# Attention and gated LoRA layer on one core: mask and maximum in one VectorE pass per head, third group's probabilities normalized by VectorE

## The reference, cut to what matters

```python
x = x + attn(layernorm(x), wq, wk, wv, wo, q_norm_w, k_norm_w)
x = x + ffn(layernorm(x), weight, gate_w, lora_U, lora_V)

# attn: 16 heads of 64, 4 key/value heads, window of 128 tokens
q, k = rmsnorm(q), rmsnorm(k)
scores = einsum("bqhd,bkhd->bhqk", q, k) / sqrt(64)
scores = where((i >= j) & (i - j < 128), scores, -inf)
y = einsum("bhqk,bkhd->bqhd", softmax(scores), v) @ wo.T
# ffn: 8 experts of rank 16
gate = softmax(xt @ gate_w.T)
out = xt @ weight.T + einsum("ne,eor,ner->no", gate, lora_V, t) / 16
```

## Time and profile before

| | |
|---|---|
| median of the runs | 2353.57 us (2352.46 to 2354.76, 3 runs) |
| the profiled execution | 2355.66 us |
| its span, first to last instruction | 2353.9 us |
| TensorE matmuls busy | 2311.7 us, 98% |
| VectorE busy | 2129.8 us, 90% |
| ScalarE busy | 2051.7 us, 87% |
| GpSimd busy | 1262.7 us, 54% |
| mean granted TensorE clock | 0.997 |

### The profile page before, as it was taken

How to read it: one execution, slowest core, us unless ns; L and a number is a source line. 1 busy time by engine, 2 the same in 40 slices (tenths; PEclk the granted TensorE clock), 3 DMA queues, 4 the chain that set the end, 5 groups by cost and what they waited for, 6 DMA issues and landing times.

```text
span 2353.9 us, 117523 instructions
## 1 busy us (share of the span) xinstructions
PE 2311.7 (98%) x49424; PEld 1979.1 (84%) x49424; DVE 2129.8 (90%) x5871; ACT 2051.7 (87%) x7175; POOL 1262.7 (54%) x1644
## 2 busy tenths in 40 slices
PE   6999999999999999999999999999999999999998
PEld 4888888888888888888888888888888888888886
DVE  6899999999999999999999999999999999999996
ACT  5888888898888988888888889888888888898886
POOL 2555555555555555555555555555555555555553
PEclk9999999999999999999999999999999999999999
DMA  2000000000000000000000000000000000000000
GB/s 73 12 17 21 17 16 17 21 16 17 21 17 17 17 21 17 17 17 21 17 16 21 17 16 17 21 17 17 17 21 17 16 18 20 17 16 21 17 10 14
DMA packets 39913, 44.25 MB, mean 19 GB/s; under 512 B 4448, under 2 KB 38624, under 8 KB 39392
## 3 DMA queue, kind: packets, MB, share of 16 engines
q1 hardware_dynamic: 39392, 36.73, 5.0%
HBM read 19.93 MB, written 16.78 MB: 16 GB/s over the span
## 4 chain that ended last, share of the span: by engine, by line
PE 75%; ACT 14%; DVE 9%; issue 1%; POOL 0%; DMA 0%; SPq 0%; DVEq 0%
PE ps_a L676 9%; PE ps_scores L721 9%; PE ps_y L743 7%; PE ps_d L670 5%; ACT probs L345 5%; PE ps_d L672 5%; PE ps_d L671 5%; PE ps_y L756 4%; PE ps_c L676 4%; PE ps_y L773 4%; PE ps_b L670 3%; PE ps_b L672 3%; PE ps_b L671 3%; DVE gate L577 2%; PE ps_b L676 2%; ACT qT L333 2%
## 5 line engine op out<-in xcount | busy, mean ns | idle before, releaser
L345 ACT ACTIVATE probs<-merged,neg_max 128x128 f32<-128x128 f32 x2048 | 801.2, 396 | 102.8 <-DVE neg_max L515 99.5
L242 POOL TENSOR_TENSOR q_r<-q_ve,minus_half 128x8 f32<-128x8 f32 x256 | 420.3, 1642 | 264.2 <-DVE q_ve L491 257.9
L345 ACT ACTIVATION_READ_ACCUMULATOR probs<-merged,neg_max 128x1 f32 x2048 | 397.3, 194 | 0.0
L721 PE MATMUL ps_scores<-kT,qT 64*32 64x160 f32 (+4 forms) x16384 | 377.5, 281 | 5.4 <-DVE merged L509 4.2
L515 DVE TENSOR_REDUCE neg_max<-merged 128x4 f32<-128x512 f32 x512 | 343.7, 671 | 0.1
L264 POOL TENSOR_SCALAR_AFFINE_SELECT pT_other<-pT 128x256 f32<-128x256 f32 x384 | 159.5, 415 | 342.7 <-ACT pT L352 338.8
L352 ACT ACTIVATE pT<-ps_a 128x512 f32<-128x512 f32 x512 | 307.6, 601 | 12.0 <-PE ps_a L676 1.6
L676 PE MATMUL ps_a<-ident,probs 128*128 128x128 f32 x2048 | 314.8, 276 | 1.1 <-DVE probs L526 0.6
L670 PE MATMUL ps_d<-wo_h,yT_h 128*128 128x256 f32 x1024 | 310.4, 303 | 0.7 <-ACT qT L333 0.7
L672 PE MATMUL ps_d<-wo_l,yT_h 128*128 128x256 f32 x1024 | 288.0, 281 | 0.0
L671 PE MATMUL ps_d<-wo_h,yT_l 128*128 128x256 f32 x1024 | 287.6, 281 | 0.0
(11 more groups left out here) (119 smaller groups left out, 6347.4 us busy)
## 6 DMA issues: line engine op xcount, KB each, us to landing
xs<-x SPq DMA_DIRECT2D x128, 128.0 KB, 2.1
out<-ob SPq DMA_DIRECT2D x128, 128.0 KB, 2.1
w_plain<-w_qkv SPq DMA_DIRECT2D x3, 512.0 KB, 4.9
w_plain<-w_o SPq DMA_DIRECT2D x8, 128.0 KB, 5.4
w_plain<-w_ffn SPq DMA_DIRECT2D x1, 392.0 KB, 6.2
w_plain<-w_v SPq DMA_DIRECT2D x1, 128.0 KB, 5.1
nw<-norm_w SPq DMA_DIRECT2D x1, 1.0 KB, 5.4
```

The lines of the kernel that those rows point to most:

```text
L242: pool.tensor_tensor(q_r[:, T % DEEP, c], q_ve[:, T % DEEP, c], minus_half[:, 0:8], ALU.pow).then_inc(s_qr[n], 1)
L345: last = nc.scalar.activation(probs[:, r, h], merged[:, r, h], ACT.Exp, bias=neg_max[:, r, h:h + 1], accum_out=den[:, r, h:h + 1])
L721: last = nc.tensor.matmul(ps_scores[queries, 2 * half + c, first:end], qT[rows, T % 2, 2 * g + c, queries], kT[rows, g // 2, at + first:at ...
```

## The change

For tiles of slot 0, `merge` becomes one `tensor_tensor_reduce` for each of the four heads. It writes the negated masked scores, -(scores + neg_later), to `merged` and their minimum over the keys, which is the negated maximum, to `neg_max`. `maximum` no longer runs for these tiles, and `exps` waits for `s_merged` instead of `s_max` and undoes the sign with scale -1. The semaphore `s_max` counts the tiles of slot 1 to 3 alone.

`NORM_BY_POOL` becomes empty: the normalization of group 2 leaves GpSimd for VectorE, in all 128 tiles, and stands between `high_value_difference(T)` and `gate_share(T - 3)`.

```diff
-NORM_BY_POOL = (2,)
+NORM_BY_POOL = ()
@@ gpsimd, step
                 q_power(T + 2, 0)
-                norm_by_pool(T, 2)
                 select(T, 1)
@@ scalar, exps
-                    act.wait_ge(s_max, groups(T, g))
+                    if slot(T):
+                        act.wait_ge(s_max, later_groups(T, g))
+                    else:
+                        act.wait_ge(s_merged, groups(T, g))
                     for h in heads:
-                        last = nc.scalar.activation(probs[:, r, h], merged[:, r, h], ACT.Exp, bias=neg_max[:, r, h:h + 1], accum_out=den[:, r, h:h + 1])
+                        last = nc.scalar.activation(probs[:, r, h], merged[:, r, h], ACT.Exp, bias=neg_max[:, r, h:h + 1], scale=1.0 if slot(T) else -1.0,
+                                                    accum_out=den[:, r, h:h + 1])
@@ vector, merge
                         dve.wait_ge(s_s, groups(T, g))
-                        nc.vector.tensor_tensor(merged[:, ring(T, g)], ps_scores[:, :, P:2 * P], neg_later[:].unsqueeze(1).to_broadcast(every),
-                                                ALU.add).then_inc(s_merged, 1)
+                        r = ring(T, g)
+                        for h in range(REP):
+                            last = nc.vector.tensor_tensor_reduce(merged[:, r, h], ps_scores[:, h, P:2 * P], neg_later[:], -1.0, -MASKED, ALU.add, ALU.min,
+                                                                  accum_out=neg_max[:, r, h:h + 1])
+                        last.then_inc(s_merged, 1)
@@ vector, maximum
-                if live(T):
+                if live(T) and slot(T):
@@ vector, step
                 high_value_difference(T)
+                norm_probs(T - 1, 2)
                 gate_share(T - 3)
```

## The result

The changed kernel takes 2341.86 us (median, 2341.73 to 2342.51, 5 runs) against 2353.57 us before: a ratio of 0.995, 95% interval 0.9937 to 0.9963, so 11.7 us faster. Predicted were 2342.6 us and a gain of 11.

What follows compares the result with a forecast made beforehand. TensorE's matmuls bound the kernel; only its stalls, 0.62 us a sequence, were winnable. Saving 0.08 + 0.17 + 0.17 - 0.05 = 0.37 over 32 sequences gives 12 us, less 1: 11 off 2353.57, so 2342.6 us; range 2339 to 2366.

Steps and rivals of the forecast that it cites:

- What bounds the kernel: TensorE's matmuls bound each step; the main loop wait is its L743 weight loads for VectorE's `yT_l`, 34.3 us.
- The ceiling, 20 us: L743 stalls of 0.08, 0.27 and 0.27 us a sequence, 20 us over 32 sequences, are all other engines can give back.
- `gate` is blocked by GpSimd's pass: On VectorE, slots 1 to 3: GpSimd's third-group normalization holds up `gate`, 0.89 us instead of 0.13, costing 0.76 us.
- 0.65 in place of 0.82, so 0.17 each with slot 1 and 2: VectorE from `gate`'s place to the merge: pass 0.60 plus unblocked `gate` 0.05 replace 0.82 us, making `yT_l` 0.17 earlier.
- Slot 0 hides the pass: The added normalization wins nothing with slot 0; slack covers it, as `yT_l` ends at 1037.91 and TensorE wants it at 1039.13.
- x = 0.26: VectorE cost per head of the combined add and maximum, slot 0: 0.19 + 0.07 us, 1.04 for four heads.
- D: Delay of ScalarE's `g_exp` and slot 1's chain once four heads' passes exceed 0.99 us; taken as 0.05 us.
- S: TensorE's stall for `yT_l` in slot 0's first group once four heads' passes exceed 1.06 us; taken as 0.
- The sum: Saved per sequence: 0.42 - D - S = 0.37 us, 12 us over 32 sequences, less 1 us: 11 us.
- Rival C: Accumulator readouts break VectorE's overlap; beyond 0.31 us per head the kernel is slower, 2.6 us per further 0.01; chance 0.22.
- the fourth group's loss: With slot 1, `yT_l` comes late for the fourth L743 group once four heads' passes exceed 1.08 us; not in the sum.
- The rule of the emptied pipeline: Each VectorE instruction waits for the pipeline to empty, giving 0.29 + 0.16 = 0.45 us per head; the prediction sided against it.

Runs made afterwards that it cites:

- e6_gate_first: The kernel before with `gate` moved up, ahead of the reciprocal that releases GpSimd, GpSimd's pass kept: 2325.67 us against 2354.79, ratio 0.9876.
- e1_norm_only: The kernel before with only the third group's normalization moved to VectorE: 2345.06 us against 2353.46, ratio 0.9962.
- e7_gate_scalar: The kernel before with `gate` written as `tensor_scalar`, one tensor input instead of two, GpSimd's pass kept: 2353.95 us against 2354.79, ratio 0.9996.
- e12_stats_behind_x: The changed kernel with `x_statistics` alone moved behind `add_x`, the reciprocal staying ahead: 2342.23 us against 2354.06, ratio 0.9951.
- e10_x_first: The changed kernel with `gate_t` and `add_x` moved ahead of `x_statistics` and the fourth reciprocal on VectorE: 2350.46 us against 2353.26, ratio 0.999.

## Why the prediction was right, point by point

- **What bounds the kernel**: right. Only the stalls of TensorE could be won, and the gain is that of the L743 distances.
- **The ceiling, 20 us**: wrong. It counted only the longest wait for another engine in the table of waits. The wait for `x1` with slot 1 (0.17 us a sequence) is in no table. The one for `tgT_l` is in it (9.9 us, 35 times) and was passed over; it costs TensorE about 0.03 us once a sequence as long as the others stand. `e6_gate_first` won 29 us. For this change it made no difference: `x1` and TensorE both came earlier, and the distance stayed at 0.20.
- **`gate` is blocked by GpSimd's pass**: right. 0.16 us once GpSimd doesn't run it (`e1_norm_only`, the changed kernel) or `gate` stands ahead (`e6_gate_first`).
- **0.65 in place of 0.82, so 0.17 each with slot 1 and 2**: a little too much. The pass keeps 0.62 to the next instruction and the unblocked `gate` 0.07, 0.69 together; 0.13 each. With slot 3, 0.07 for 0.08.
- **Slot 0 hides the pass**: right; `yT_l` is done 0.2 us ahead of TensorE.
- **x = 0.26**: too high, it is 0.21. The readout, which I priced at 0.07 as a small instruction of its own, costs 0.03. So D is 0 where 0.05 was taken, and S is 0.
- **The sum**: 0.13 + 0.07 + 0.12 for 0.17 + 0.08 + 0.12. 0.33 instead of 0.37 a sequence, 10.4 us instead of 12. That the total came within 1 us is in part luck. With x at 0.21 my own terms would have given 0.42 a sequence, 13.4 us; the x taken too high hid about half of the 0.09 by which the gain at `gate` was overestimated. The 1 us taken off as a margin and the 1.3 us outside the loop, which I hadn't forecast, did the rest.
- **Rival C, the cliff beyond x = 0.31**: the mechanism was shown by adding passes, the slope was too flat. With six passes, 1.26 us for 4x, it would have given 2355; the run took 2363. Further meetings (`tgT_l`, the scores) were left out, and the fourth group's loss was named but priced at nothing. From six passes to eight the expected 27 us were 49.
- **The rule of the emptied pipeline** (the Trainium skill, "VectorE: DVE Perf Modes", "The DRAIN you can't avoid"), by which a head was estimated at 0.45: it doesn't hold for these passes; eight instructions take 0.84 us.

## What to carry to other kernels

A tiny instruction with a long row may be waiting and not slow: look at what the engine beside it runs at that moment, and try first to move the tiny instruction ahead of the long one instead of moving the long one's work (here 29 us against 8). Where one engine meets another several times in one unbroken stretch of work, a stall won at one meeting can come back at the next, as it did here, so list all meetings and serve them together. Measure a stall as the distance between two starts, in every kind of step, and compare it with the step where nothing is waited for; the table of waits misses those that pipelined rows cover.

## What the runs showed of the hardware

- A VectorE multiplication by one value per partition (`tensor_scalar`, 128x8, float32, SBUF to SBUF) is held up by a GpSimd pass over SBUF tensors as a `tensor_tensor` is: 0.90 us for 0.89 (`e7_gate_scalar`). A predicated copy with its scores in PSUM and its mask in SBUF is not: 0.76 us during such a pass (`e6_gate_first`).
- That GpSimd pass (128x512) took 1.28 us where VectorE ran `v_diff` as it began, and 1.04 in the steps that leave `v_diff` out.
- The combined add and minimum shows as two instructions, 0.28 and 0.08 us, and one head follows another in 0.21 us, where a plain 128x128 instruction keeps 0.18 (the changed kernel).
- A normalization right behind the reciprocal that it waits for starts 0.20 us after it, where an instruction that doesn't wait for it starts after 0.08. With others between the two, that loss is gone (`e12_stats_behind_x` against `e10_x_first`, 8 us).
